# A gated attention block with a mixture of experts: experts computed for gathered rows instead of densely

## What is computed

```python
x = x + tanh(g_xattn) * attention(layernorm(x), ctx)      # unchanged by the edit
x = x + tanh(g_ffn) * ffn(layernorm(x))

def ffn(x):                                   # E, I, K = 8, 176, 2; shared width 352
    scores = softmax(x @ gate_w.T)
    topk_w, topk_idx = top_k(scores, 2)
    topk_w = topk_w / sum(topk_w)
    y_all = einsum('eti,eih->eth', silu(x @ w1[e]) * (x @ w3[e]), w2)   # for each expert e
    y = sum(y_all[topk_idx, tok] * topk_w)
    shared = silu(x @ sw1) * (x @ sw3) @ sw2
    return y + shared
```

## Time and profile before

| | us |
|---|---|
| median of 3 runs | 1021.36 (1020.69 to 1021.43) |
| the profiled execution | 1020.03 |
| its span | 1018.3 |
| TensorE busy | 930.3 |
| VectorE, ScalarE, GpSimd busy | 760.0, 759.8, 704.2 |

### The profile page before, as it was taken

How to read it: one execution, slowest core, us unless ns; L and a number is a source line. 1 busy time by engine, 2 the same in 40 slices (tenths; PEclk the granted TensorE clock), 3 DMA queues, 4 the chain that set the end, 5 groups by cost and what they waited for, 6 DMA issues and landing times.

```text
span 1018.3 us, 21021 instructions
## 1 busy us (share of the span) xinstructions
PE 930.3 (91%) x6752; PEld 665.4 (65%) x6752; DVE 760.0 (75%) x1612; ACT 759.8 (75%) x2396; POOL 704.2 (69%) x533
## 2 busy tenths in 40 slices
PE   0375899999999999999999999999976999999998
PEld 0254677778787787778778777877733555555554
DVE  8899789888888988888988889898863833333332
ACT  3486899999999999999999999999873432222221
POOL 4597789799898888979988988888831422232322
PEclk9697899999999999999999999999997999999999
DMA  9323223333242333324233332423434100000000
GB/s 251 104 83 101 61 53 74 58 62 68 51 77 51 68 61 62 67 51 77 51 69 60 59 70 51 77 51 71 112 64 118 59 1 22 1 21 0 21 0 21
DMA packets 183265, 63.12 MB, mean 62 GB/s; under 512 B 167248, under 2 KB 180912, under 8 KB 183232
## 3 DMA queue, kind: packets, MB, share of 16 engines
q1 hardware_dynamic: 179120, 60.62, 27.3%
q0 software_dynamic: 4112, 2.10, 1.5%
HBM read 20.76 MB, written 2.10 MB: 22 GB/s over the span
## 4 chain that ended last, share of the span: by engine, by line
PE 59%; issue 16%; DVE 10%; POOL 6%; ACT 5%; DMA 1%; SPq 1%; POOLq 0%; DVEq 0%; ACTq 0%
PE S L426 10%; PE A L329 7%; PE A L330 7%; PE T L397 5%; POOL pT L1458 5%; PE JB L456 5%; PE S L414 4%; PE VB L321 3%; PE VB L323 2%; PE VB L322 2%; PE T L447 2%; DVE stage L977 1%; ACT zq L637 1%; DVE zq L935 1%; PE T L322 1%
## 5 line engine op out<-in xcount | busy, mean ns | idle before, releaser
L1346 POOL TENSOR_TENSOR rstd<-var,mhalf 128x8 f32<-128x8 f32 (+1 forms) x128 | 191.1, 1509 | 76.7 <-DVE var L1054 76.3
L329 PE MATMUL A<-w_hi,xq 128*128 128x256 f16 (+1 forms) x1024 | 187.4, 249 | 35.4 <-DVE v_lo L1028 20.5
L1458 POOL TENSOR_TENSOR pT<-zq,pT 128x512 f16<-128x512 f32 (+1 forms) x56 | 65.3, 1165 | 181.9 <-ACT pT L865 174.3
L330 PE MATMUL A<-w_lo,xq 128*128 128x256 f16 (+1 forms) x1024 | 187.4, 249 | 0.0
L426 PE MATMUL S<-kT,qT 128*128 128x256 f32 x512 | 142.1, 401 | 8.5 <-ACT kT L732 4.3
L870 ACT ACTIVATE qT<-A 128x512 f32<-128x512 f32 (+1 forms) x56 | 33.4, 596 | 152.2 <-PE A L323 152.2
L1040 DVE TENSOR_SCALAR qT<-T,qmap 128x512 f32<-128x512 f32 x128 | 103.6, 809 | 55.5 <-PE T L397 55.5
L1012 DVE TENSOR_REDUCE nmx<-S 128x2 f32<-128x512 f32 (+1 forms) x192 | 114.7, 598 | 28.0 <-PE S L426 25.6
L329 PEld LDWEIGHTS A<-w_hi,xq 128*128 128x128 f16 x1024 | 101.3, 99 | 47.0 <-issue 30.7
L743 ACT ACTIVATE prob<-S,nmx 128x256 f32<-128x256 f32 x256 | 119.3, 480 | 14.8 <-DVE nmx L1012 13.5
L1408 POOL TENSOR_TENSOR raw<-raw,rstd 128x1024 f32<-128x1024 f32 x64 | 126.3, 1974 | 0.0
(11 more groups left out here) (187 smaller groups left out, 2599.4 us busy)
## 6 DMA issues: line engine op xcount, KB each, us to landing
stage<-wallT SPq DMA_DIRECT2D x8, 1024.0 KB, 4.9
wp<-wpT POOLq DMA_DIRECT2D x1, 2048.0 KB, 30.5
out<-v_lo SPq DMA_DIRECT2D x8, 256.0 KB, 2.2
xs<-x SPq DMA_DIRECT2D x1, 1792.0 KB, 20.5
pT<-psrc SPq DMA_TRANSPOSE x64, 4.9
sq<-w2s SPq DMA_DIRECT2D x7, 128.0 KB, 3.1
sq<-w1T SPq DMA_DIRECT2D x3, 256.0 KB, 3.3
sq<-w3T SPq DMA_DIRECT2D x3, 256.0 KB, 3.2
```

What stands on the lines that cost most here:

```text
L329: nc.tensor.matmul(o, l, w_hi[:, c, col:col + n], start=(c == 0), stop=False)
L330: last = nc.tensor.matmul(o, l, w_lo[:, c, col:col + n], start=False, stop=(c == HC - 1))
L1346: return nc.gpsimd.tensor_tensor(dst, src, mhalf[:, 0:n], ALU.pow)
L1458: nc.gpsimd.tensor_tensor(a_lo[0:n, j % 3, :], act_b[0:n, j % 2, :], a_hi[0:n, j % 3, :], ALU.subtract).then_inc(f_alo, 1)
```

## The change

The experts are computed sparsely. Each of the 4096 pairs of a token and an expert gets a slot; each expert's slots are padded to whole tiles of 128, so that 39 tiles hold every routing (4096 + 8 x 127, divided by 128).

- The normalised tokens z are stored to memory (`zd`) during attention, one transfer of 256 KB for each sequence, on SyncE's queue (`store_z`).
- The rank of each pair within its expert comes from matmuls with a triangle of ones (`rank_early`, `carry_early`, `rank_late`), and the list of tokens by slot from 32 matmuls with two one-hot tiles each (`table`), which VectorE writes (`marks`, four instructions for each of 16 token tiles). VectorE counts and places the tiles (`count_tiles`, `plan_tiles`).
- For each of the 39 tiles, GpSimd gathers 128 rows of z (`fetch_z`), TensorE turns them (`turn_z`), ScalarE and VectorE split them, TensorE reads the expert's number into a register and takes the weights from there (`expert_up`, 6 matmuls with 352 columns), then Silu and the product, TensorE turns it again (`turn_a`), it is split, and `expert_down` makes 6 matmuls with 256 columns. ScalarE copies the result out, and SyncE stores it (`yd`).
- The shared expert has 3 tiles of columns for 4 blocks, 12 steps: six of them ahead of the expert tiles, six behind (`M0`).
- At the end GpSimd gathers for each of 16 token tiles two tiles of rows of `yd` (`fetch_y`, 32 gathers), and VectorE adds them, weighted, to x (`mix`).
- The weights come in 5 units: the shared expert (2176 columns with its down part), then two experts each (1408 columns on 128 rows and 1024 on 88).

The core of the diff:

```diff
-IT = E * I + SHARED
-FC = -(-IT // P)
+HE = I // 2
+FS = -(-SHARED // P)
+MS = NBLK * FS
+M0 = MS // 2
+NTL = (2 * B * S + E * (P - 1)) // P
...
 # SyncE
             for n in range(1, STEPS - 4):
                 flip(n)
+                if n % G == 4 and n > G:
+                    store_z(n // G - 1)
...
+            for j in range(NTL):
+                done(sp, e_y, j)
+                sp.dma_start(yd[j * P:(j + 1) * P, :], yo[:, j % 3, :]).then_inc(st_y[j % 3], 16)
...
 # TensorE
+            def expert_up(j):
+                ...
+                e = pe.value_load(expert[0:1, j:j + 1], min_val=0, max_val=E - 1)
+                done(pe, e_zl, j)
+                done(pe, e_a, j - 2)
+                o = (S0, S1)[j % 2][:, 0:2 * I]
+                for c in range(HC):
+                    wh, wl = (w[:, c, bass.ds(e * (2 * I), 2 * I)] for w in (w13_hi, w13_lo))
+                    zh, zl = (zt[:, j % 2, k, c * P:(c + 1) * P] for k in range(2))
+                    last = split3(o, zh, zl, wh, wl, start=(c == 0), stop=(c == HC - 1))
+                last.then_inc(e_up, 1)
...
+            for j in range(NTL + 2):
+                if j + 1 < NTL: turn_z(j + 1)
+                if j < NTL: expert_up(j)
+                if 0 <= j - 1 < NTL: turn_a(j - 1)
+                if 0 <= j - 2 < NTL: expert_down(j - 2)
+            for m in range(M0, MS):
+                shared_up(m)
+                if m - 2 >= M0: shared_down(m - 2)
...
 # ScalarE, drain of step 2
-                        ffn_tick(0, 1)
+                        shared_silu(1)
+                        shared_high(0)
...
 # VectorE
+            def marks(t):
+                ...
+                for k in range(2):
+                    nc.vector.tensor_scalar(ring[:, t % NR, k, 0, :], kc[:, K_IOTA:K_IOTA + P], rlo[:, t, k:k + 1], None, ALU.is_equal)
+                    last = nc.vector.tensor_scalar(ring[:, t % NR, k, 1, :], kc[:, K_COL:K_COL + P], col[:, t, k:k + 1],
+                                                   kc[:, K_TOK + t:K_TOK + t + 1], ALU.is_equal, ALU.mult)
+                last.then_inc(f_oh, 1)
+            def mix(q):
+                done(dve, f_fin, 2 * q // BT)
+                dve.wait_ge(ld_yk[q % (NG // 4)], 64 * (q // (NG // 4) + 1))
+                ...
 # GpSimd
+            def fetch_z(j):
+                ...
+                done(pool, e_zt, j - 3)
+                pool.indirect_dma_start(zg[:, j % 3, :], None, zd, bass.IndirectOffsetOnAxis(ap=tokidx[:, j:j + 1], axis=0)
+                                        ).then_inc(ld_zg[j % 3], 16)
...
+            exps(1, NE, NT)
+            for j in range(NTL): fetch_z(j)
+            shared_low(M0)
+            shared_low(M0 + 1)
+            for i in range(2 * NT):
+                fetch_y(i)
+                if i % 6 == 3 and M0 + 2 + i // 6 < MS: shared_low(M0 + 2 + i // 6)
```

More of the change, by code:

```diff
@@ new lines, in _ @@
+            done(pe, ta_z, B - 1)
+            transpose_tokens(zf, ta_T, JB)
+            for t in range(12, NE): table(t)
+            shared_up(5)
+            carry_early()
+            shared_down(3)
+            done(pe, ta_lo, B - 1)
+            logits(NT - ST, NT, VB, R_LG - (NT - ST) * E, False).then_inc(f_lgm, 1)
+            shared_down(4)
+            rank_late()
+            shared_down(5)
+            for t in range(NE, NT): table(t)
+            pick_tokens()
+            turn_z(0)
@@ L1112, in tick @@
                         low_px(n0 - 3, par(3))
-                        ffn_tick(0, 1)
-                        weights(0, 0, NT - ST)
-                    if g >= 3:
+                        shared_mul(1)
+                        mix_weights(0, 0, NE)
+                    if g == 3:
+                        whole_out(n0 - 5, par(5))
+                        shared_mul(2)
+                        ranks(0, 0, NE, T0)
+                        for t in range(4): marks(t)
+                    if g == 4:
                         whole_out(n0 - 5, par(5))
@@ new lines, in _ @@
+            tail1(B - 1)
+            for t in range(4, 8): marks(t)
+            shared_mul(3)
+            ffn_low(2)
+            for t in range(8, 12): marks(t)
+            finish(0)
+            ffn_low(3)
+            for t in range(12, NE): marks(t)
+            shared_mul(4)
+            tail_low(B - 1, JB)
+            shared_mul(5)
+            ffn_low(4)
+            read_logits(1, NE, NT, VB, R_LG - NE * E)
+            for k in range(2): best(1, NE, NT, k)
+            members(NE, NT)
@@ new lines, in _ @@
+            ranks(1, NE, NT, VB)
+            count_tiles()
+            for t in range(NE, NT): marks(t)
+            plan_tiles()
+            read_table()
+            read_tokens()
+            finish(1)
+            mix_weights(1, NE, NT)
+            low_z(0)
+            for j in range(NTL + 1):
+                if j + 1 < NTL: low_z(j + 1)
+                if j < NTL: expert_mul(j)
+                if 0 <= j - 1 < NTL: low_a(j - 1)
+                if j == 4: slots()
+            shared_mul(M0)
@@ L1343, in _ @@
+            shared_mul(M0 + 1)
+            mix(0)
+            shared_mul(M0 + 2)
+            mix(1)
+            shared_mul(M0 + 3)
+            finish(2)
+            mix(2)
+            shared_mul(M0 + 4)
+            mix(3)
+            shared_mul(M0 + 5)
+            mix(4)
+            mix(5)
+            finish(3)
+            for q in range(6, NT // 2): mix(q)
         @block.gpsimd
```

731 lines of the change are left out of this document (433 added, 298 removed).

## The result

| | before | after |
|---|---|---|
| median of the runs, us | 1021.03 (1020.26 to 1021.43, 4 runs) | 1026.58 (1025.76 to 1027.43, 4 runs) |
| span of the profiled execution, us | 1018.3 | 1023.9 |
| mean granted clock | 0.973 | 0.939 |

The ratio is 1.0055, 95% interval 1.0038 to 1.0073: half a per cent slower, where 3% faster was predicted. Busy time by stretch answers the earlier trace rows; the columns are the same (busy us and instructions of PE, PEld, DVE, ACT, POOL; clock, DMA share, GB/s). The stretches are attention, most of the router, 80 us of the sparse tiles, and the end.

A forecast was written before the change was run, and what follows sets the result against it. TensorE's time from about 750 us was taken as the bound. Router 47, first gather 5, sparse tiles 101, shared half and gathers back 64 make 217 instead of 239, from a start 8.5 earlier: 991 us, range 955 to 1052.

The forecast's parts named there:

- two are 1.0, half hidden: Sparse tiles, TensorE's queue: two register loads at 0.5 us each, half hidden, giving 2.5 us a tile.
- the hole closes: Before the router: TensorE's near-idle time from 768.4 to 779.47 vanishes, so group 3's work starts at 771.
- 3 for waits: Router, VectorE's list: 3 us of waits on TensorE added to 43.7 us of work, 47 us in all.
- SyncE's queue ("nothing"): Attention: seven stores of z between transposes can delay one only by their issue, 0.5 us, and cost nothing.
- the prediction's other half: End: gathers only write descriptors, so they would leave VectorE's mixes alone; four mix ops 1.9 us.
- the queue's rate of 0.025 us: Sparse tiles: TensorE's queue takes a matmul with its load every 0.025 us, 0.4 a tile, so can run ahead.
- The register rival: Sparse tiles: exposed register loads set the pace; 3.2 us a tile eats the gain, 4.0 gives 1052; chance 0.20.
- GpSimd's queue has two low halves: Before the gathers back: two shared-expert low halves stand first on GpSimd, 7.7 us, to 932.
- four more low halves between them: End, GpSimd: four low halves at 1.16 us between 32 gathers at 1.4, together 49.5 us, to 981.5.
- The rival with dear gathers: Gathers cost 1.9 us: still under 2.5 in the loop, +16 at the end, 1007 us; chance 0.14.
- The one with cheap gathers (1.0): Register loads fully hidden (2.05 a tile, -18) and gathers at 1.0 us (-13): 960 us; chance 0.20.
- The clock: Sparse tiles: at a granted 1.2 GHz a tile takes 3.9 us, giving 1048 us; chance 0.07.

The follow-up runs named there:

- both runs that shorten it: Changed kernel with shared tile 2's multiply moved behind the ranks: 1022.07 us; changed kernel with TensorE's up tile 5 and ScalarE's high half 4 moved earlier: 1021.47 us.
- the kernel with all edits: Changed kernel plus one register load, multiply behind ranks, two waits removed, shared weights earlier, end's low halves on VectorE with mixes earlier: 959.44 us, ratio 0.9396.

## Why the prediction was wrong, step by step

The forecast was 991 us, faster by 30; measured were 1026.58, slower. Three steps failed: "two are 1.0, half hidden" for the register loads (they cost the whole 1.0 us a tile), "the hole closes", and "3 for waits" in the router (they were 10.3). The sum of the prediction ends at a span of 988; it is 1023.9. The 35.9 us lie here:

| step | predicted | measured | miss |
|---|---|---|---|
| group 3's work on VectorE starts | 771 | 778.3 | +7.3 |
| router, to the token list | 47 | 55.2 | +8.2 |
| token list to first up matmul (839.2) | 5 | 5.7 | +0.7 |
| sparse tiles, to the last row of y (956.5) | 101 | 117.3 | +16.3 |
| from there to the first gather back | 8 | 9.0 | +1.0 |
| gathers back | 49.5 | 51.7 | +2.2 |
| last landing, mix, store | 6.5 | 6.7 | +0.2 |

No single step turns the sign. The sparse tiles, the router and its start together are 31.8 us, just more than the 30 of the forecast; by this sum the kernel would have been faster with any one of the three as predicted.

**Up to the router.** "The hole closes" failed. The prediction followed only the wait that ended the hole before, unit 2's weights, and asked of VectorE's own edits what they cost; it did not follow the next instruction in line, a multiply of the shared expert that waits through GpSimd for attention's last product. The run with the multiply behind the ranks shows it: 4.5 us. That product was itself late, by 6.9 us against the +2.2 of the prediction. The delay grows along the chain: VectorE's low half of unit 0 stood at 745.89, before at 742.92, and ScalarE's table load at 754.71 instead of 750.41. The term that failed is SyncE's queue ("nothing"): it asked only what issue costs, and unit 0's second part, issued at the same time as before, landed 2.35 us later, with 681 KB more ahead of it. The last of the seven stores of z is 256 KB of these. The stores ahead of it cost nothing: the transposing DMA of 730.20 stands at 729.74.

**The router.** That VectorE's list sets its length held; both runs that shorten it shorten the whole. The bare work was well sized: marks 0.9 us a tile where 0.8 was put, low halves 2.75 instead of 3.0. The 3 us for waits were mis-sized: 1.94, 1.69, 3.05 and 2.91, and two of 0.3 to 0.4, are 10.3 us. Four marks took 1.06 to 1.18 us instead of 0.28 to 0.34 beside a GpSimd instruction (792.98 in VectorE's timeline, with GpSimd on the normalisation of z):

```profile
792.98 1.06 DVE L1458 TENSOR_SCALAR xq<-w_lo,ctx_lo 128x128 f16<-128x128 f32 x1
```

The Trainium skill (SBUF — State Buffer, Who interferes with whom), which the prediction had used for instructions with two SBUF inputs, also names tensor_scalar, the operation of the marks, as one that can take both port pairs and can then contend with GpSimd. The four rows agree; which mode the marks ran in no run here shows. The mixes at the end, with two SBUF inputs, answer the prediction's other half: seven of eight took 1.79 to 1.82 us for their four operations, with gathers beside them, and the eighth 3.32 us, beside a low half on GpSimd (1002.98 and 1003.53 in the timelines).

**Sparse tiles.** This is the largest miss: without it the sum would be 991 + 19.6 = 1011, still faster. The price of TensorE's work was right (1.99 with no load, against 2.0). "Two are 1.0, half hidden" was not: unhidden, they were the whole 1.0. The argument for hiding was the queue's rate of 0.025 us and waits that are met a tile earlier; one load a tile costs little (0.16), as that argument would have it, but with two it fails. The register rival had the mechanism and the place; the point from which it decides, 3.2 us a tile, was worked out with all other terms as predicted. With 3.0 a tile and these it gives 991 + 40.5 x 0.5 = 1011 us; together with the late router it is slower. The Trainium skill (DMA: Bandwidth & Descriptors, Latency and other measured facts) puts a register load at about 600 ns at least; the kernel with four loads agrees with it for a load right behind another, since in most tiles where TensorE is at full speed the way from the turns to the up tile's first matmul grows from 0.73 to between 1.34 and 1.44 us. The 0.5 us that the queue stands for each load of the changed kernel, and the 0.16 of the kernel with one, are only what isn't covered, and show no whole duration.

**Gathers.** The price was put at 1.4 us, between 0.95 and 1.9; it was 0.95 busy and 1.25 from one to the next. The 5 us that this gave were lost again: "GpSimd's queue has two low halves ahead" was right and cost 1 us more, and "four more low halves between them" was taken at their own 1.16 us. But each of them can close a ring: low half on GpSimd, behind ScalarE's high half, behind VectorE's multiply, behind a mix on VectorE that waits for gathers on GpSimd. It cost 7.5 us of idle time, 5.04 at the first and 2.50 at the second.

The rival with dear gathers is out. The one with cheap gathers (1.0) had GpSimd's busy time right but not the 1.25 us from one to the next, and the loads wrong. The clock did not decide (0.99 in the loop).

**Where the gain of the sparse form went.** 44 dense tiles of 4.32 us were 190 us; the sparse ones take 117, 73 less. All the rest took 239 - 190 = 49 us before, and now takes 128: router and first gather (833.5 - 778.3 + 5.7 = 61 us) and the end (1023.9 - 956.5 = 67 us). In the kernel with all edits sparse tiles, router with first gather, and end are 86, 57 and 51 us (first up matmul at 821.5, last row of y at 907.7), and the form wins.

## What to carry to other kernels

Price an instruction on a queue that sets the pace with nothing hidden, and don't take the price of one for that of two: one register load a tile cost 0.16 us, the second 0.83. Keep a loaded register instead of loading it again. Ask of a transfer how many bytes stand ahead of it, and not only when it is issued: here it was issued on time and landed 2.35 us late. When a wait is removed, read off the same queue which instruction comes next and follow its own releasers, through other engines, to the end; here it was 8 us away. Do not put work that waits for a consumer onto the queue that feeds this consumer: low halves between gathers cost 15.5 us until they and the mixes were reordered. Nor put a multiply that waits ahead of ranks that could run: 4.5 us.

## What the runs showed of the hardware

- An indirect transfer of 128 rows of 1 KB holds GpSimd 0.95 us, the next one starts 1.25 us after it, and the instruction that waited for the rows started 2.7 to 3.4 us after the start of the last gather it needed. Gathers from z and from y cost the same.
- Register loads on TensorE's queue: 0.16, 0.83 and 0.58 us for the first, the second, and each of two more of a tile.
- VectorE's 128-column compare with scalars: 0.28 to 0.34 us, beside an elementwise GpSimd instruction up to 1.18. Four accumulations with two inputs there took 1.79 to 1.82 us beside gathers and 3.32 beside a GpSimd subtraction.
- With four loads a tile TensorE's granted clock fell to 0.85 on average and matmuls ran at 1.2 GHz in places (352 columns 0.29 us apart); with two its mean was 0.99.
- In the profiled execution of one kernel ScalarE stood 15.96 us, and TensorE up to 2.19 us between matmuls, for nothing that the profile names. Not explained.
